# Decoder layer on one core: the products of a head's five lower levels move behind the norms of the head ahead

## The reference

```python
q = _l2norm((x @ Wq).reshape(Bb, Tt, H, DK))
k = _l2norm((x @ Wk).reshape(Bb, Tt, H, DK))
v = (x @ Wv).reshape(Bb, Tt, H, DV)
alpha = jax.nn.sigmoid(x @ Wg).reshape(Bb, Tt, H, DK)
def step(S, qkva):
    q_t, k_t, v_t, a_t = qkva
    S = a_t[..., None] * S + k_t[..., None] * v_t[:, :, None, :]
    o_t = jnp.einsum('bhkv,bhk->bhv', S, q_t)
    return (S, o_t)
...
return o @ Wo
```

## Time and profile before

| | |
|---|---|
| median of three executions | 492.22 us (490.24 to 492.79) |
| the profiled execution | 491.47 us, span 489.7 us |
| granted TensorE clock, mean over the span | 0.989 |
| busy TensorE / its weight loads | 467.3 us (95%) / 384.3 us (78%) |
| busy VectorE / ScalarE / GpSimd | 361.2 us (74%) / 337.6 us (69%) / 108.0 us (22%) |
| DMA | 20.15 MB, mean 41 GB/s |

### The profile page before, as it was taken

One profiled execution on the slowest core, in us unless ns is written; L12 is line 12 of the kernel. 1 busy time (PEld: TensorE's weight loads), 2 busy tenths in 40 slices (PEclk: granted clock), 3 DMA queues, 4 the chain that ended last, 5 costly groups with the idle time before them and its releaser, 6 DMA issues.

```text
span 489.7 us, 23902 instructions
## 1 busy us (share of the span) xinstructions
PE 467.3 (95%) x10242; PEld 384.3 (78%) x10242; DVE 361.2 (74%) x1036; ACT 337.6 (69%) x797; POOL 108.0 (22%) x102
## 2 busy tenths in 40 slices
PE   1799999999999999999999999999999999999986
PEld 1588788887888888878888888877888888877674
DVE  5777887656679788885759788887578769786564
ACT  3858776766777876777856776777957786866613
POOL 1022222202222222231222220323222211232121
PEclk9989999999999999999999999999999999999979
DMA  8900000001001010013011010003010001002013
GB/s 321 343 5 5 3 5 3 5 3 46 3 5 46 3 46 4 4 47 89 3 47 46 3 46 4 4 25 105 8 46 4 3 9 40 4 25 67 1 47 125
DMA packets 15272, 20.15 MB, mean 41 GB/s; under 512 B 1216, under 2 KB 12992, under 8 KB 15168
## 3 DMA queue, kind: packets, MB, share of 16 engines
q1 hardware_dynamic: 13888, 14.43, 9.0%
q0 software_dynamic: 1280, 4.20, 3.1%
HBM read 16.53 MB, written 2.10 MB: 38 GB/s over the span
## 4 chain that ended last, share of the span: by engine, by line
PE 57%; DVE 6%; ACT 3%; issue 2%; POOL 1%; DVEq 0%; ACTq 0%
PE ring L1179 15%; PE acc L1292 8%; PE lo_bank L1203 6%; PE ring L1192 6%; PE ring L1273 4%; PE ring L1343 2%; PE hi_bank L1262 2%; PE ring L1280 2%; PE ring L1301 1%; PE hi_bank L1234 1%; PE hi_bank L1242 1%; PE ring L1532 1%; PE ring L1310 1%; PE ring L1361 1%; PE ring L1353 1%
## 5 line engine op out<-in xcount | busy, mean ns | idle before, releaser
L485 ACT COPY states<-states 128x512 f32<-128x512 f32 x128 | 80.9, 632 | 47.7 <-DVE states L709 32.3
L397 POOL TENSOR_TENSOR rnorm<-norm_sq,neg_half 128x4 f32<-128x4 f32 x32 | 45.1, 1408 | 265.0 <-DVE norm_sq L772 265.0
L709 DVE TENSOR_TENSOR states<-states,spans 128x512 f32<-128x512 f32 x96 | 66.5, 692 | 8.1 <-ACT states L485 0.9
L1203 PEld LDWEIGHTS lo_bank<-states 128*32 128x32 f32 x5120 | 50.9, 110 | 22.9 <-issue 19.1
L1292 PE MATMUL acc<-wo_sb,oT_sb 128*128 128x256 f32 x256 | 60.8, 380 | 0.9 <-ACT oT_sb L512 0.9
L1203 PE MATMUL lo_bank<-states 128*32 128x16 f32 (+1 forms) x5120 | 57.7, 188 | 0.0
L760 DVE COPY_PREDICATED blocks<-owned,lo_bank 128x64 f32<-128x64 uint32 (+1 forms) x160 | 41.0, 257 | 22.2 <-PE lo_bank L1203 17.6
L1192 PE MATMUL ring<-wv_sb,xnT 128*128 128x256 f32 x384 | 55.7, 295 | 0.9 <-DVE wv_sb L965 0.9
L1179 PE MATMUL ring<-xnT,wk_sb 128*128 128x512 f32 x192 | 53.7, 416 | 2.0 <-DVE xnT L828 1.6
L1179 PE MATMUL ring<-xnT,wq_sb 128*128 128x512 f32 x192 | 53.4, 413 | 0.0
L1179 PE MATMUL ring<-xnT,wg_sb 128*128 128x512 f32 x192 | 51.3, 403 | 0.6 <-DVE wg_sb L965 0.3
(11 more groups left out here) (193 smaller groups left out, 774.7 us busy)
## 6 DMA issues: line engine op xcount, KB each, us to landing
x_buf<-x_dram SPq DMA_DIRECT2D x4, 512.0 KB, 3.9
ctxT_sb<-ctxT_dram SPq DMA_DIRECT2D x8, 256.0 KB, 3.7
ctx_sb<-ctx_dram SPq DMA_DIRECT2D x4, 512.0 KB, 3.8
out_dram<-x_mid SPq DMA_DIRECT2D x6, 256.0 KB, 2.6
states<-wk_dram SPq DMA_DIRECT2D x1, 1024.0 KB, 5.7
states<-wg_dram SPq DMA_DIRECT2D x1, 1024.0 KB, 7.8
states<-wq_dram SPq DMA_DIRECT2D x1, 1024.0 KB, 9.8
v_sb<-wv_dram SPq DMA_DIRECT2D x1, 1024.0 KB, 11.9
```

What stands on the lines that cost most here:

```text
L397: nc.gpsimd.tensor_tensor(rnorm[:, m % 4, GB:2 * GB], norm_sq[:, GB:2 * GB], neg_half[:, GB:2 * GB], ALU.pow).then_inc(rk_set, 1)
L485: nc.scalar.copy(halves(l, 2 ** (l - 1), False), halves(l - 1, 2 ** (l - 1), False)).then_inc(carry_set, 1)
L709: nc.vector.tensor_tensor(halves(l, w, True), halves(l - 1, w, True), by, ALU.mult).then_inc(decayed, 1)
L1203: last = mm(lo_bank[BLOCK * r:BLOCK * r + BLOCK, to:to + columns], view(states, left + start, [[1, BLOCK]]), view(states, right + start, q ...
```

## The change

For heads 1 to 31, RUNS[0] and RUNS[1] move from their two places within the head to its very beginning, ahead of tail_part "S" and v, and so directly behind RUNS[2] and norms of the head ahead. Head 0 keeps its order. Products, operands, waits, banks and the order of the ring stay as they are.

```diff
             for n in range(U):
+                if n > 0:
+                    levels(n, RUNS[0])
+                    levels(n, RUNS[1])
                 tail_part(n, "S")
                 project_v(n)
                 if n + 1 < U:
                     project(wg_sb, ("g", n + 1)).then_inc(g_mm, 1)
-                levels(n, RUNS[0])
+                if n == 0:
+                    levels(n, RUNS[0])
                 if n + 1 < U:
                     project(wq_sb, ("q", n + 1)).then_inc(q_mm, 1)
                 if n >= 2:
                     attend_transposed(n - 2)
                 if n + 2 < U:
                     project(wk_sb, ("k", n + 2)).then_inc(k_mm, 1)
-                levels(n, RUNS[1])
+                if n == 0:
+                    levels(n, RUNS[1])
                 tail_part(n, "A")
```

## The result

The changed kernel takes 607.12 us (median of 4 runs, 600.24 to 613.12) against 491.96 us (490.24 to 492.79): 1.230 times as long, with a 95% interval from 1.225 to 1.235. The run of 613.12 us was in a slower state of the chip, and the ratio rests on the other three, whose median is 605.56. The prediction said 490.8 us with a range up to 498.5. No rival reached that far either; the nearest was E, the clock, with 53 us and a chance of 0.03.

A forecast was written before the change was run, and what follows sets the result against it. TensorE's own order of work was taken to set the time. Fewer switches -16.7 us, losses +2.4, +5.3, +4.5, +0.9 and +2.2, sum -1.4 from the median of 492.22: 490.8 us, range 483.0 to 498.5.

The forecast's parts named there:

- E, the clock: Rival: each head's short stretch lowers TensorE's granted clock once, 31 x 1.7 = 53 us lost; chance 0.03.
- Does a product stay as cheap in a stretch of 256 records?: Joined short products behind the norms: no surcharge, judged by a 192-record stretch in head 0; bound 2.5 us in all.
- D: Rival: the stretch of short products slows with its length, 0.08 to 0.3 us per head, 493 to 500 us; chance 0.08.
- TensorE issues all the time: Argument against a falling clock: TensorE has no idle gaps between bursts; the 192 records at 33.08 kept 1.00.
- The two switches fewer: Per head, two entries and two exits between long and short products fall away: 0.54 us, times 31 heads 16.7 us.
- rival (F): Rival: switches between long and short products cost nothing real, so only the losses stay, 507 us; chance 0.03.
- What moves: Shifted starts of v, g, q, k and deadlines in each head: losses of 2.4, 5.3, 4.5, 0.9 and 2.2 us.
- attend waits 1.55 us for the squares: Heads 11, 19, 27: v_scaled's chain moves by 1.2, 1.0 and 1.5 us, so the head grows; loss 5.3 us.
- The transposes: Heads 12, 20, 28: later layer norm moves them by 1.08 in head 12, 0.6 us of slack in the others.
- Level 4's operands: Plain heads: decays end 11.9 us after the norms, against a deadline of 12.69; 0.8 us to spare.
- C: Rival: the gate chain does not fit plain heads either; 0.5 us beyond the reserve is 7.5 us, 498 us; chance 0.16.

The follow-up runs named there:

- row of 512 products: Kernel before, with 512 short products going round four strips of the bank, once, ahead of the loop over heads: 520.08 us (one run).
- run with two stretches of 128: Kernel before, from head 1 with level 0 behind the norms and levels 1 to 4 behind g, two stretches of 128 records per head: 498.59 us, ratio 1.012.
- 587.59 us run: Kernel before, plus one TensorE wait per head from head 1, between norms and v, until the norms' squares are taken: 587.59 us, ratio 1.194.
- 549.03 us run: Kernel before, with 512 short products all writing one strip of the bank, once, ahead of the loop over heads: 549.03 us (one run).

## Why the prediction was wrong

**The step that failed** is "Does a product stay as cheap in a stretch of 256 records? I take no surcharge; the bound is [...] 2.5 us in all." It cost about 80 us in standstills and brought the half clock with it, where 116 us stand between forecast and result. The bound came from the one stretch of 192 records in the trace of before, and that row had a particular reason to be clean: by the same count it holds a single boundary, at 34.38 us, and the packet for the piece behind it had begun at 31.21, 3.2 us ahead, while the long matmuls of q ran. 192 records are 384 instructions and can do with one boundary; 256 are 512 and always hold two, 1.2 us apart. The row was read as "a long stretch is harmless"; it only said "this one was". Between 60 and 449 us the pieces of before last 3.97 us at least, 5.5 on average, above the 3.45 us at which the row of 512 products stood still at each boundary. The order of before had its short products spread just thinly enough.

The Trainium skill has the mechanism ("Runtime: NRT & Kernel Launch", section "Instruction fetch mechanics"): an engine's program streams through a FIFO in 16 KiB blocks of 256 instructions, which the traces here agree with (81 packets of 16 KB, gaps 128 records apart). I had not drawn on it. It would have misled me on the size: it calls the fetch hidden by the pace of issue and gives TensorE room for 2048 instructions, where the row of 512 products stood still at each 256. The measurement decides.

**D** had the right place (256 records in over 2.6 us without a wait, which was to show it) and the wrong size and form: 0.08 to 0.3 us per head, spread over the records, against 2.1 us in one piece.

**E, the clock** ("31 x 1.7 = 53 us would be lost", chance 0.03) came true in part, and behind the standstills, not by itself: 88.7 us at 1.2 GHz cost at most half of that, 44 us. Nine of the 29 periods of the changed kernel have no such piece in them. Without idle time six of them are 0.17 to 0.42 us shorter than before, the other three 0.09 to 0.32 longer. With all 29 like the nine, or like the six, the growth without idle time would have been -3 to -8 us; it was 30.1, so by this estimate the half clock costs 33 to 38 us. I argued against E that "TensorE issues all the time". That premise is what broke. What lowers the clock is not settled in full: idle time of 2 us per head does it alone (587.59 us run), and a row of short products without any pause holds it at 1.2 GHz as well (549.03 us run). How the two share the loss in the changed kernel stays open.

**The two switches fewer** were right as far as can be seen. The same six periods are 0.17 to 0.42 shorter; adding 0.17 for the modelled end ahead of a gap, that is 0.34 to 0.59 where I had 0.54. The other three do not show the gain. The prediction's rival (F), switches that cost nothing, falls by the six and by the heads of the run with two stretches of 128.

**What moves** was right where it could still be seen. The time lines of heads 11 and 12:

```profile
208.88 1.16 PE L1273 MATMUL ring<-v_sb,attnT 128*128 128x128 f32 x8 [1.55 <-ACT squares L458]
...
228.91 1.09 PE L1301 MATMUL ring<-ident,xn 128*128 128x128 f32 x8 [0.90 <-DVE xn L695]
```

attend waits 1.55 us for the squares in heads 11, 19 and 27, which is 1.04, 1.04 and 1.46 more than before; I had 1.2, 1.0 and 1.5. The transposes wait 0.90, 0.52 and 0.53 us; I had 1.08, and 0.6 of slack off it twice. Level 4's operands came in time in plain heads. That does not settle C, since the heads were some 3 us longer and gave the gate chain that time too. Nearly all of this lies in the shade of the standstills.

## What to carry to other kernels

Price a move of small instructions by how long 256 instructions of that engine take at their new place, weight loads counted, not by the price of one. Where 256 held less than some 3.4 us of work here, the engine mostly waited for its own program; it did not where the packet for the next 256 had started early enough, as 3.2 us ahead of 34.38 us in the kernel before. The profile shows such a wait as idle time ended by "issue" without a releaser, at a fixed step of the instruction count, with one packet on the instruction queue each. To read such a wait, shift it: a few harmless instructions ahead of the loop tell at once whether it belongs to the place in the loop or to the count. And a clean row bounds a cost only if it contains what could go wrong; ask what it leaves out before it is scaled up.

## What was not expected of the hardware

- TensorE's program comes in packets of 16 KB for 256 instructions. In the row of 512 products that goes round four strips a piece took 3.45 us: the packet started 1.04 to 1.12 us after a piece was entered, the next piece began 2.33 to 2.41 us after that. In the changed kernel the shortest piece ahead of a standstill took 3.18 us.
- Short products (32 columns of weights, 1 to 64 moving) take 9 ns a record when they go round four strips of a bank's rows (13.3 at 1.2 GHz), and 31.8 ns (53.3 at 1.2 GHz) when all write one strip. 128 columns of weights and 1 moving column take 112 ns.
- The granted clock fell to 1.2 GHz 15 times between 36 and 450 us where TensorE stood still for about 2 us or more in each head (587.59 us run), and it stayed there through 52.4 us of short products without a pause (549.03 us run). There it came back within some us of long matmuls: the window from 83.50 us, 5.5 us after the short products, is at 1.00.
